# A graph network on one core: setup records in f16 and in smaller groups, one-hots in planes, and other node groups

## The reference, cut to what matters

```python
agg = segment_sum(x[src], dst)                            # layer 0: plain sum over edges
x = layernorm(x + x @ Wres + bres + relu((x + agg) @ W1 + b1) @ W2 + b2)
# layer 1, twice: h = relu(((h + mean over edges of h[src]) @ Wa.T + ba) @ Wb.T + bb)
# layer 2, four steps: x += 0.1 * tanh(x @ A.T + segment_sum(norm * (x @ Wphi.T)[src]) + self term + bias)
#   norm = dinv[src] * dinv[dst] * edge_weight, dinv = 1/sqrt(weighted degree + 1)
# layer 3: relu(segment_sum((x @ W + b)[src] + edge_attr @ We + be))
```

## Time and profile before

| | |
|---|---|
| median of 3 runs | 1177.41 us (1174.58 to 1179.05) |
| the profiled execution | 1174.85 us |
| its span, first to last instruction | 1173.0 us |
| PE busy | 1044.1 us, 89% |
| DVE busy | 543.5 us, 46% |
| ACT busy | 274.7 us, 23% |
| DMA | 310.57 MB, mean 265 GB/s |

### The profile page before, as it was taken

How to read it: one execution, slowest core, us unless ns; L and a number is a source line. 1 busy time by engine, 2 the same in 40 slices (tenths; PEclk the granted TensorE clock), 3 DMA queues, 4 the chain that set the end, 5 groups by cost and what they waited for, 6 DMA issues and landing times.

```text
span 1173.0 us, 25340 instructions
## 1 busy us (share of the span) xinstructions
PE 1044.1 (89%) x10553; PEld 619.7 (53%) x10553; DVE 543.5 (46%) x1061; ACT 274.7 (23%) x558; POOL 67.8 (6%) x69
## 2 busy tenths in 40 slices
PE   0335888888869999999999999999999999999998
PEld 0234677777655555545445554465544645445454
DVE  4398799999473336522312223222322314444333
ACT  0246698888520000000000000000000002112100
POOL 3811000000000000000000000000000000000000
PEclk9865799999999999999999999999999999999999
DMA  6405476767798675777766987669886698753951
GB/s 190 104 12 157 202 299 287 300 287 300 328 367 349 236 303 222 268 304 312 262 254 227 386 354 284 233 247 382 337 305 222 258 385 324 306 203 145 427 193 31
DMA packets 40520, 310.57 MB, mean 265 GB/s; under 512 B 12138, under 2 KB 15069, under 8 KB 18581
## 3 DMA queue, kind: packets, MB, share of 16 engines
q1 hardware_dynamic: 29528, 299.34, 65.0%
q0 software_dynamic: 8416, 9.50, 2.9%
q10 hardware_dynamic: 2522, 0.98, 0.4%
HBM read 244.49 MB, written 65.26 MB: 264 GB/s over the span
## 4 chain that ended last, share of the span: by engine, by line
PE 75%; DMA 12%; DVE 5%; issue 3%; ACT 2%; ACTq 2%; SPq 0%; DVEq 0%
PE ps L1193 45%; PE ps L1183 17%; DMA weight_mats<-arena 11%; PE ps L1142 4%; PE ps L1304 2%; PE ps L1279 2%; PE ps L1097 2%; PE ps L1155 1%; ACTq L908 1%; DMA edge_table<-arena 1%; ACTq L911 1%; DVE arena L665 1%; PE ps L1124 0%; DVE stats L673 0%; ACT arena L930 0%
## 5 line engine op out<-in xcount | busy, mean ns | idle before, releaser
L1193 PE MATMUL ps<-arena 125*128 125x500 f32 (+1 forms) x700 | 268.5, 539 | 0.0
L1193 PE MATMUL ps<-arena,parts_even 125*128 125x500 f32 (+1 forms) x700 | 267.6, 538 | 0.0
L1193 PEld LDWEIGHTS ps<-arena 125*128 125x128 f32 x700 | 123.3, 190 | 127.8 <-issue 127.8
L1193 PEld LDWEIGHTS ps<-arena,parts_even 125*128 125x128 f32 x700 | 122.9, 189 | 127.4 <-issue 127.4
L948 ACT ACTIVATE XT<-ps 128x500 f32<-128x500 f32 (+1 forms) x49 | 26.6, 543 | 517.8 <-PE ps L1155 517.8
L1183 PE MATMUL ps<-arena 125*128 125x500 f16 (+2 forms) x700 | 140.8, 352 | 3.8 <-issue 3.2
L1304 PE MATMUL ps<-arena 64*128 64x52 f16 (+1 forms) x6500 | 106.5, 181 | 36.5 <-DVE arena L665 21.7
L962 ACT ACTIVATE arena<-ps 128x400 f16<-128x400 f32 (+1 forms) x195 | 124.1, 636 | 38.6 <-PE ps L1304 24.0
L1304 PEld LDWEIGHTS ps<-arena 64*128 64x128 f16 x6500 | 96.4, 95 | 54.3 <-ACT arena L964 30.8
L964 ACT ACTIVATE arena<-ps 128x400 f32<-128x400 f32 (+1 forms) x195 | 116.6, 598 | 0.0
L660 DVE TENSOR_TENSOR arena<-arena 128x4224 f16<-128x4224 f16 (+2 forms) x52 | 116.2, 2235 | 0.0
(11 more groups left out here) (176 smaller groups left out, 710.6 us busy)
## 6 DMA issues: line engine op xcount, KB each, us to landing
arena<-weight_mats SPq DMA_DIRECT2D x24, 3250.0 KB, 11.4
arena<-weight_mats SPq DMA_DIRECT2D x24, 3000.0 KB, 10.9
arena<-count_mats SPq DMA_DIRECT2D x18, 3125.0 KB, 13.2
weight_mats<-arena SPq DMA_DIRECT2D x13, 3125.0 KB, 14.4
count_mats<-arena SPq DMA_DIRECT2D x13, 1562.5 KB, 6.0
arena<-weight_mats SPq DMA_DIRECT2D x4, 1625.0 KB, 7.2
arena<-weight_mats SPq DMA_DIRECT2D x4, 1500.0 KB, 6.3
arena<-count_mats SPq DMA_DIRECT2D x3, 1562.5 KB, 6.2
```

The lines of the kernel that those rows point to most:

```text
L1193: ins = t.matmul(o, xs[:, k, :], rhs, start=(k == 0), stop=(k == NC - 1))
```

## The change

- **Records** are f16, in six groups of 3, 3, 5, 5, 5 and 4 chunks, each taken as its gathers land; what DVE does on x and weights now stands between the groups. hi and lo are rounded by way of two f32 scratch tiles. The degrees are reduced group by group instead of at the end, the largest weight is taken from `t_w` while DVE waits for the first gather of windows, and four constants are made there too. PE's 52 transposes become f16 matmuls with an f16 identity, batches 0 to 3 ahead of the transposes of weights, 4 to 7 ahead of the weight products, 8 to 15 behind them; the last four batches share a bank. Three copies of transposed weights and two of products go from DVE to ACT. The three `bcol` DMAs go from ACT's queue to SP's, behind x.
- **One-hots**: `hot_lo` has three planes for half a pair (67 or 58 targets). `produce` makes `eq` for a half, the hi one-hot of its first step, both weight planes in one operation, and then the hi one-hot of its second step. The first pair is made once 4 batches of columns are there.
- **Groups** of 4, 4, 4, 4, 4, 3 and 2 chunks. Both matrices are stored chunk by chunk instead of pair by pair, so that a load takes runs of 6250 bytes for counts and 6000 or 6500 for weights, and a store two runs to a partition where it had one.

The diff, cut to its core:

```diff
-GROUPS = -(-NC // GRP)
+GROUP_AT = (0, 4, 8, 12, 16, 20, 23, NC)
+GROUPS = len(GROUP_AT) - 1
-CG = 5
+REC_AT = (0, 3, 6, 11, 16, 21, NC)
-        count_mats = nc.dram_tensor("count_mats", (PAIRS, 128, NC * 2 * NP), F16).ap()
-        weight_mats = nc.dram_tensor("weight_mats", (PAIRS, 128, NC * 2 * NP), F32).ap()
+        count_mats = nc.dram_tensor("count_mats", (PAIRS, 2, 128, NC * NP), F16).ap()
+        weight_mats = nc.dram_tensor("weight_mats", (PAIRS, 2, 128, NC * NP), F32).ap()
-        hot_lo = [at(83704 + 14008 * i, 128, [STEP_MAX, 3 * LO], F16) for i in range(2)]
+        hot_lo = [at(92408 + 10452 * i, 128, [3, HALF_MAX, LO], F16) for i in range(2)]
-        ring_c = [at(25000 * i, 128, [2, NC, 2 * NP], F16) for i in range(RING)]
+        ring_c = [at(25000 * i, 128, [GRP, NC, NP], F16) for i in range(RING)]
...
+            def records(i):
+                cs, n = slice(REC_AT[i], REC_AT[i + 1]), REC_AT[i + 1] - REC_AT[i]
+                dve.wait_ge(sd_in[i], 16 * n)
...
+                v.tensor_tensor(cnt, sdw[:, cs, :, 1], d_c[:, cs].to_broadcast([NP, n, SLOTS]), ALU.is_equal)
+                link(v.tensor_scalar(hi32[:, 0:n, :], source, 1.0 / NC, -0.5 + 0.5 / NC, ALU.mult, ALU.add))
                 v.tensor_tensor(wm, weight, cnt, ALU.mult)
+                link(v.tensor_scalar(hi, hi32[:, 0:n, :], ROUND_MAGIC, -ROUND_MAGIC, ALU.add, ALU.add))
+                v.tensor_copy(w1, wm[:, :, 0:last])
+                link(v.scalar_tensor_tensor(lo32[:, 0:n, :], hi, -float(NC), source, ALU.mult, ALU.add))
+                v.tensor_reduce(S8[:, cs, 0], cnt, AX, ALU.add)
+                v.scalar_tensor_tensor(lo, lo32[:, 0:n, :], 1.0, cnt[:, :, 0:last], ALU.add, ALU.mult)
+                v.tensor_tensor(w2, wm[:, :, 0:last], w1, ALU.subtract).then_inc(rec_ok, 1)
+                link(v.tensor_reduce(S8[:, cs, 1], wm, AX, ALU.add))
+            records(0)
+            records(1)
...
+            records(2)
+            dve.wait_ge(round_ok, 1)
+            v.scalar_tensor_tensor(parts_even[:, 1], Xn[:, :, :], X_SCALE, parts_even[:, 0], ALU.mult,
+                                   ALU.subtract).then_inc(parts0_ok, 1)
+            records(3)
...
+            records(4)
...
+            records(5)
...
-            def produce(q, u):
+            def produce(q, half):
...
+                t0, n, u = HALF_AT[half], HALF_AT[half + 1] - HALF_AT[half], 2 * half
+                eq = hot_lo[half][:, 0, 0:n, :]
+                wait_used(u)
+                v.tensor_tensor(eq.rearrange("p t (a j) -> p t a j", j=2), numbers(iota_lo, n, LO),
+                                code(lo_c[:, bass.ds(q, 1), t0:t0 + n, :], LO), ALU.is_equal).then_inc(eq_ok, 1)
+                rows_hot(u)
+                dve.wait_ge(eq_ok, 2 * q + half + 1)
+                both = w_c[:, bass.ds(q, 1), t0:t0 + n, :, :].rearrange("p q t k j -> p (q t k) j")
+                v.tensor_tensor(hot_lo[half][:, 1:3, 0:n, :].rearrange("p k t m -> p t k m"),
+                                eq.unsqueeze(2).to_broadcast([128, n, 2, LO]),
+                                both.unsqueeze(2).to_broadcast([128, 2 * n, LO // 2, 2]), ALU.mult).then_inc(hots_ok, 1)
+                wait_used(u + 1)
+                rows_hot(u + 1).then_inc(hots_ok, 1)
...
-                dve.wait_ge(col_ok, 16)
+                dve.wait_ge(col_ok, 4)
+                for half in range(2):
+                    produce(0, half)
+                dve.wait_ge(col_ok, 16)
+                with dve.Fori(1, PAIRS) as q:
+                    for half in range(2):
+                        produce(q, half)
...
-            for i, k in enumerate(("L0_b1", "L1_b1a", "L1_b2a")):
-                act.dma_start(bcol[:, i:i + 1], w[k].rearrange("(d o) -> d o", o=1),
-                              allow_slow_non_contiguous=True).then_inc(w_in, 16)
...
+            def record_rows(b):
...
+                    ins = t.matmul(record_bank(b, n)[:, j * NP:j * NP + NP],
+                                   rec[k][:, 2 * q:2 * q + 2, :].rearrange("p c s -> p (c s)"), ident16[0:NP, 0:NP],
+                                   start=True, stop=True)
```

More of the change, by code:

```diff
@@ L78, in chunks_of, with groups_to, recs_to @@
 def chunks_of(g):
-    return min(GRP, NC - GRP * g)
+    return GROUP_AT[g + 1] - GROUP_AT[g]
+def groups_to(k):
+    return sum(a < k for a in GROUP_AT[:-1])
+def recs_to(k):
+    return sum(a < k for a in REC_AT[:-1])
 def layer_of(r):
@@ L361, in _ @@
             sp.dma_start(Xn[:, :, :], x.rearrange("(p c) f -> p c f", c=NC)).then_inc(x_in, 16)
+            for i, k in enumerate(("L0_b1", "L1_b1a", "L1_b2a")):
+                sp.dma_start(bcol[:, i:i + 1], w[k].rearrange("(d o) -> d o", o=1),
+                             allow_slow_non_contiguous=True).then_inc(w_in, 16)
             sp.wait_ge(consts, 2)
@@ L621, in _ @@
-            dve.wait_ge(rec_ok, NC // CG)
-            v.tensor_reduce(flags[0:NP, 1:2], cntR[:, 0:NC, last], AX, ALU.max)
-            link(v.tensor_reduce(flags[0:NP, 2:3], w_max, AX, ALU.max))
-            link(v.tensor_scalar(flags[0:NP, 2:3], flags[0:NP, 2:3], WEIGHT_MAX, None, ALU.is_gt))
+                hi, lo, w1, w2 = (r_[:, cs, 0:last] for r_ in rec)
+                cnt, wm = cntR[:, cs, :], w_slots[:, cs, :]
+                v.tensor_tensor(cnt, sdw[:, cs, :, 1], d_c[:, cs].to_broadcast([NP, n, SLOTS]), ALU.is_equal)
@@ L1243, in _ @@
             pe.wait_ge(flag_ok, 1)
-            pe.wait_ge(xt0_ok, GROUPS)
-            t.matmul(ps[0:1, 6, 0:1], flags[:, 0:1], one_col[:, :], start=True, stop=True).then_inc(flag_ps, 1)
+            pe.wait_ge(w8_ok, 1)
+            t.matmul(ps[0:1, SUM_BANK, 0:1], flags[:, 0:1], one_col[:, :], start=True, stop=True).then_inc(flag_ps, 1)
             def spread_degrees(g):
@@ L1255, in spread_degrees @@
                 ins.then_inc(rep_ps, 1)
-            def spread_w8():
-                t.matmul(ps[:, SUM_BANK, 0:D], eights[:, :], W8[:, :],
-                         start=True, stop=True).then_inc(w8_ps, 1)
             def fast():
@@ L1300, in pair @@
                             o, e = 2 * LO * (T - UNIT_AT[u]), T - STEP_AT[step]
+                            half = step // 2
+                            e_lo = T - HALF_AT[half]
                             for a, z in ((0, 2), (2, 3)):
```

325 lines of the change are left out of this document (161 added, 164 removed).

## The result

The changed kernel takes 1190.34 us (median of 4 runs, 1184.43 to 1192.29) against 1176.89 us of the kernel before beside it: a ratio of 1.0109, 95% interval 1.0079 to 1.0139. It is slower by 1.1%. The forecast was 1166 us, with 1150 to 1180 as its range: a gain was forecast, and the change loses time. The profiled execution takes 1188.94 us, its span is 1187.1 us, 14.1 more than before.

A forecast was written before the change was run, and what follows sets the result against it. No engine was taken as full before layer 2: setup a serial path, building paced by stores of weights, layer 2 by PE. Setup -13.0, building +12 and rounds -8.4 gave -9.4 on 1174.85, forecast as 1166 us, range 1150 to 1180.

The forecast's parts named there:

- The ring: Building: DVE and PE take turns on one-hots, 16.7 to 16.9 us a pair against 15.83; +12 us over 12 pairs.
- In the ring PE idles twice a pair, 1 to 2 us: Building: length of PE's two waits for DVE in each pair, 1 to 2 us.
- the clock: Rival, building: PE's clock drops to 1.2 GHz after waits, +3 us a pair, 1202 us if all twelve; chance 0.11.
- Groups 0 to 2 fit ahead of it, in time in which DVE waits: Setup: DVE makes the first three groups' records in idle time before L555, which starts at 47.8 us.
- the floor: Setup: the last gather, landed at 65.8 us, limits how early the records can end.
- ACT is no longer late for PE's transposes: Setup: PE's 3.52 us wait for ACT goes; x's f16 part on ACT ends at 47.8 us.
- ACT's last batches: Setup: ACT's 8 more column batches are ready at about 78.5 us, hidden with 1.4 us to spare.
- the hole ahead of round 7: Rounds: PE's 2.54 us wait for counts at the start of round 7 disappears, -2.5 us.
- the start of round 1: Rounds: PE's 1.04 us wait for the layer norm of group 5 goes, -1.0 us.
- loads in shorter runs are slower: Rival, layer 2: transfers a third longer would make PE wait; middle priced at 1185 us; chance 0.07.
- The stores stay the limit: Rival, building: the stores still set the pace at 15.83 us a pair, no ring cost, 1154 us; chance 0.22.
- gathers held up by the records: Rival, setup: DVE's record operations delay gathers up to 4.5 us beyond the 1.5 taken, 1170 us; chance 0.12.

The follow-up runs named there:

- e6: The changed kernel with ten useless 512-column matmuls on PE ahead of its wait for step 0 of each pair; 1175.78 us, ratio 0.9991.
- e8: e3 with x's load held until the first six gathers have landed; 1165.43 us, ratio 0.9904.
- e13: e3 with x's load split in two, 112 and 13 rows; 1151.83 us, ratio 0.9819.
- e3: The changed kernel with eq and both weight planes made ahead of the wait for the hi buffer; 1157.27 us, ratio 0.9833.
- e4: e3 with the groups of before, six of 4 chunks and one of 1; 1167.6 us, ratio 0.9924.
- e11: e3 with x's load issued earlier, right behind the store of the table; 1160.58 us, ratio 0.986.
- e12: e3 with x's load issued earlier still, ahead of the store of the table; 1163.14 us, ratio 0.988.
- e5: e3 with the three bcol loads back on ACT's queue; 1158.55 us, ratio 0.9842.
- e10: e8 with the work on x moved back behind records and first columns, plus six useless PE matmuls a pair; 1165.38 us, ratio 0.991.
- e14: e13 plus six useless 512-column PE matmuls in the wait for step 0 of each pair; 1154.38 us, ratio 0.9821.

## Why the prediction was wrong

The span grew by 14.1 us where the forecast took 9.4 off. Of these 23.5 us 17.3 lie in the building, 4.8 in the setup and 1.4 in the rounds.

**Building, the step that decided.** It was forecast at +12 us and measured +29.3. The ring was right in form and size: DVE's first half was put at 5.25 us and is 0.99 + 2.33 + 1.97 by its rows, PE's waits came where they were said to, and with the clock held up a pair takes 16.98 us against 16.7 to 16.9 forecast. The step that failed is "In the ring PE idles twice a pair, 1 to 2 us" and, with it, the cost of PE's steps behind these waits, which the sum took at the upper clock. The forecast named the clock as a rival, priced it at +3 us a pair if every pair were hit, and gave it 0.11, because "in most pairs the clock came through waits of over 1 us". Those were waits of the kernel before.

The ring makes one long wait a pair, and its length could be worked out beforehand: step 0 is signalled 5.25 us after PE ends step 2, and step 3 fills 100 x 0.0145 + 1.18 = 2.6 of them, by the forecast's own prices. It is 3.05 us, nearly twice the longest of before, and it came back in every pair. That costs 18.42 - 16.98 = 1.44 us a pair (e6 against the change). The price of the rival was twice too high as a mean, since in most pairs only step 0 runs slowly; its chance was too low for a wait of that length. The Trainium skill, "TensorE: Matmul & The Clock Gate", section "HAM oscillation — how this bites in real kernels", by which waits between bursts bring the low clock back each time, told the likelier story: the clock fell in ten of ten pairs.

In the ten pairs from the third store to the thirteenth the ring is worth 11.5 us (16.98 - 15.83 a pair) and the clock 14.4. Another 2.6 us lie at the end of the building, where layer 0's last 50 matmuls began 2.16 us ahead of the thirteenth store and now begin 0.48 behind it, and 0.7 in the first pairs; neither was forecast. That makes 29.2 of the 29.3. The first two pairs together lost only those 0.7, where the forecast counted the ring twelve times.

**Setup, -8.2 instead of -13.0.** `mode` came at 77.16 instead of 73.3, and the first unit 7.65 behind it instead of 6.6. The step that failed is "Groups 0 to 2 fit ahead of it, in time in which DVE waits". It read the landing times as 3.6 to 4.5 us and passed over the 11.9 beside them; nothing waited for the early gathers then. Now DVE does, and they land with x (e8: 7.4 us sooner without it; e13: 4.6 us sooner with x in two). Three groups and x's reduce take 14.9 us on DVE (40.23 to 55.09), so for L555 at 47.8 the first record had to begin by 33; it began at 40.23. Groups were also sized short: 3.28 us for three chunks (40.23 to 43.51) and 4.7 to 5.1 for five, against 4.15. From the last records to `mode` the forecast was too long: 2.4 us (PE's transposes at 74.72, `mode` at 77.16) against 4.0, and its own sum gives 68.9 + 4.0 = 72.9, not 73.3.

With x in two the floor is the last gather, as forecast, and the first unit at 78.96 is 0.9 from the 79.9 of the prediction (on e3's one-hots, whose first unit comes 6.7 us behind `mode`; with the change's 7.65 it would be 79.9). "ACT is no longer late for PE's transposes" failed as well: PE waited 3.39 us for ACT's copies of x, though without a cost, since DVE took up its part of x only at 55.09. And DVE waited 2.16 us behind `mode`, 1.0 more than in e3 (1.13). The kernel says why: PE frees the hi buffers only once ACT has copied twelve batches of columns (the semaphore `sums_ok`), the change's first `eq` waits for that, and e3's does not. The forecast had called ACT's last batches hidden. The gathers' own slowdown was right in size: 4.01 us for one beside L622, little for the others.

**Rounds, -7.0 instead of -8.4.** By e4, where all but the groups is alike, they are worth 8.1 us: rounds 1 and 2 4.1 (forecast 4.4), the hole ahead of round 7 2.7 (2.5), round 7 1.1 (0.5), layer 2 2.3 (0), less 2.1 at the start of round 1, where the forecast had a gain of 1.0. There the clock is low again: the change's first ten matmuls of 500 columns took 3.52 us, and 2.3 a group later. The change as a whole gains 7.0 over the kernel before: rounds 1 and 2 2.9, layer 2 with the hole 4.8, less 0.2 ahead of round 1 and 0.5 in round 7. With the old groups e4 loses 0.6 in rounds 1 and 2 and 1.4 in round 7 against the kernel before; the new layout's 0.1 us a group is part of that. So the mis-sized terms are the start of round 1 (-1.0, measured +0.2), rounds 1 and 2, and round 7 (-0.5, measured +0.5); the unforecast gain of layer 2 makes up for most of it. The rival "loads in shorter runs are slower" was right in sign and harmless: by the medians of the two kernels a load of counts for four chunks lands in 14.5 us instead of 13.2, one of weights in 11.8 instead of 11.4, far from the third that by its own estimate it would take for PE to wait, and stores of weights in 14.5 and 14.4.

**The other rivals.** "The stores stay the limit" was wrong for the change, yet it is what e3 makes true: 16.07 us a pair. The rival of gathers held up by the records had no part in it: the last gather starts at 61.54, 1.0 later than before, within the 1.5 taken.

## What to carry to other kernels

When several short operations become one long one, ask first what the long one must wait for: here `eq` and the weight planes were put behind a buffer that only the hi one-hot needed, and moving one wait turned +1.1% into -1.7%. When two engines take turns, work out how long each will stand idle, and do not judge the granted clock by shorter waits or by its mean: three of ten pairs lost it before, all ten behind the longer wait. Before work is moved up to "as it lands", ask what its transfer shares the DMA engines with: a late landing that nobody waited for shows only as a maximum.

## What was not expected of the hardware

- Ten useless matmuls of 512 columns in each pair made the kernel 14.6 us faster, because the granted clock stayed at 1.00 instead of a mean of 0.88 (120 to 300 us).
- A load of 1.6 MB in 125 rows is there for PE 19 to 21.5 us after its issue in ten of the kernels, the one before among them, whether it is issued at 2.9, 18 or 33.7 us, and after 26.5 us in e11, where it ran beside the store of the table and the windows' load. With nothing but it and another 125-row load in flight the DMA share was 0.31 to 0.32 (e12). Gathers issued beside it land up to 15.6 us after their issue, a load of node numbers after 22. In 112 and 13 rows it lands in 12.8 us, and no gather then takes over 4.1 us.
- Issuing is held up too: two of ACT's DMAs for `brow` took 5.61 and 6.51 us to issue in e3, and 0.59 and 0.28 in e8, where x came later. In e5 the two long ones, 6.14 and 6.20, were others in the same place of the queue.

Open: why neighbours wait for nearly the whole of x rather than share with it (the gathers are in 125 rows like x, and e12 shows two such loads within one five-sixteenths share; no run gave the gathers another row count), and how much of the low clock at the start of round 1 could be had back; e10 and e14 move it too little to tell.
